# One slot of 512 edges in each edge stage fetched row by row by ScalarE's DMAs instead of GpSimd's gathers

## The chip, the cores and the metric

The kernel runs on one core of one Trainium2 chip. The metric is the device time of one execution in microseconds. Every profile here is of one execution; its span runs from the first to the last instruction, and the execution's own time is a little longer.

## What the kernel computes

A graph network of four layers over 6250 nodes of 128 features and 100,000 edges that are sorted by destination. `x` is normalised per row and clipped at zero; two layers of the first kind follow, then a residual, the same normalisation, two layers of the second kind and a last residual.

```python
def _gine_layer(x, src, dst, edge_attr, W1l, b1l, gl, bl, W2l, b2l):   # layers 0 and 1
    msg = relu(x[src] + edge_attr)
    agg = segment_sum(msg, dst, num_segments=6250)
    h = (x + agg) @ W1l + b1l
    h = (h - mean(h)) * rsqrt(var(h) + 1e-5) * gl + bl
    return relu(relu(relu(h) @ W2l + b2l))

def _gin_conv(x, edge_index, wA, bA, wB, bB, eps):                      # layers 2 and 3
    agg = segment_sum(x[src], dst, num_segments=6250)
    return relu(((1 + eps) * x + agg) @ wA.T + bA) @ wB.T + bB
```

What matters here is `x[src]` in layers 0 and 1: for each of the 100,000 edges one row of 512 bytes is fetched from a table of node rows in DRAM, and the edge's own 512 bytes are added to it.

## The kernel before, in words

Layers 0 and 1 are the two edge stages. Each walks over all edges in 49 turns (`TURNS`) of four slots (`SLOTS`); a slot is 512 edges, four (`EPP`) on each of 128 partitions. The turns are numbered through both stages, 0 to 97; `n % TURNS` is the turn within its stage. For each slot:

- **GpSimd** (line 566) issues four gathers. Each is an indirect DMA that fetches 128 rows, one per partition, by a column of row numbers from `src_all`. Two turns of buffers (`xg`) exist; before each half of a turn GpSimd waits until the sums of the same half two turns earlier are made. In the first two turns the rows come from the raw input, later from the table in DRAM, which SyncE wrote (`table_written`).
- **SyncE** loads the edges' own features for a turn (`ea`, lines 463 and 467), three turns ahead, and stores finished count units (line 482).
- **ScalarE** copies a slot's edge features into PSUM (`stage_attributes`, line 641), one slot ahead: the copy for slot i+1 is made once the sum of slot i is there. After the last slot of a half it clips both slots at zero (`messages`, line 646). After that, in turns in which a count unit is due, it casts one out of PSUM (`units_out`, line 633).
- **VectorE** adds the gathered rows to the staged features (`slot_sum`, line 968) once the copy and the gathers of that slot have landed (`gathered`). Between the sums it builds 0/1 matrices for counts (line 960), which later layers use. Between the last sum of a turn and the first of the next it adds finished windows into the accumulator (line 885), for which it reads column numbers into registers (line 907), and builds the turn's 0/1 matrix of destinations (line 932).
- **TensorE** multiplies the messages by the destinations' matrix (`edge_windows`, line 1333), one half of a turn at a time, 16 matmul instructions each, and the counts' matrices (line 1317).

After the last turn of a stage VectorE adds the last windows and the layer's two products run (line 1418 is the first). The next stage's gathers wait for the new table.

Layers 2 and 3 fetch only the edges that the counts don't cover, with indirect DMAs at line 586, and keep a tile `product` of 128 x 480 numbers for the counts' results.

The order on each engine is the program's order; an engine waits on counting semaphores. A DMA adds 16 to its semaphore when it has landed.

Of the kernel before, what the change touches and what calls it, by code (L numbers as in the profile page):

```python
# [16 lines left out]
P = 128  # L17
NODES = 6250
EDGES = 100000
D = 128  # L20
EPP = 4
SUP = P * EPP
# [3 lines left out]
SLOTS = 4  # L26
TURNS = SUPERS // SLOTS
HALVES = (range(0, 2), range(2, SLOTS))
# [7 lines left out]
GROUPS = -(-BLOCKS // GB)  # L36
# [9 lines left out]
CW = 40  # L46
# [33 lines left out]
UPG = 12  # L80
KEPT = (LEFT_PAIRS + 1) * UPG
RING = 3
CELL_RING = 6
EDGE_TURNS = 2 * TURNS
RAW_TURNS = 2
RAW_CHUNKS = SLOTS * EPP

LAYER_UNITS = [min(range(UNITS), key=lambda k: abs(2 * UNIT_END[k] - CHUNKS)) + 1, UNITS]
LAYER_CHUNKS = [0] + [UNIT_END[k - 1] for k in LAYER_UNITS]
COUNT_TURNS = TURNS - 1 - RAW_TURNS  # L90

# [9 lines left out]
def slot_chunks(n, u):  # L101

    chunks = turn_chunks(n)
    return [c for i, c in enumerate(chunks) if 1 + i * (SLOTS - 1) // len(chunks) == u]


def units_in(chunks):

    return [UNIT_OF[c] for c in chunks if c + 1 in UNIT_END]


def hots(n):
# [41 lines left out]
def gnn_kernel(nc, x, src, dst, edge_attr, W1, b1, gamma, beta, W2, b2,  # L154
               w1a, b1a, w1b, b1b, eps1, w2a, b2a, w2b, b2b, eps2, out):
    with ExitStack() as ctx:
        ctx.enter_context(nc.allow_non_contiguous_dma(reason="columns of biases"))

        def sb(name, shape, dt=F32):
            return ctx.enter_context(nc.sbuf_tensor(name, shape, dt))  # L160

        def sem(name):
            return ctx.enter_context(nc.semaphore(name))
# [4 lines left out]
        table = nc.dram_tensor("node_table", [PADDED, D], F32, kind="Internal").ap()  # L168
# [34 lines left out]
        src_all = sb("src_all", [P, SUPERS + SLOTS, EPP], I32)  # L203
# [37 lines left out]
        xg = sb("xg", [P, 2, SLOTS, EPP, D])  # L241
# [11 lines left out]
        cells = cell_room[:, 0:CELL_RING * CB].rearrange("p (r c) -> p r c", c=CB)  # L253
        counts = [cell_room[:, 0:UPG * HALF_B * CW].rearrange("p (s c) -> p s c", s=UPG),
                  hid[:, :].bitcast(F16)[:, 0:UPG * (BLOCKS - HALF_B) * CW].rearrange("p (s c) -> p s c", s=UPG)]
        product = sb("product", [P, UPG, CW])
        count_out = sb("count_out", [P, 2, CB], F16)

        xp_room = sb("xp_room", [P, BLOCKS * PARTS * D], BF16)
# [11 lines left out]
        ea = xp_room[:, RING0:RING0 + 2 * RING * SLOTS * EPP * D].bitcast(F32).rearrange(  # L271
            "p (t u j d) -> p t u j d", t=RING, u=SLOTS, j=EPP)
# [6 lines left out]
        ea_stage = psG[:, 3, 0:EPP * D]  # L279
# [36 lines left out]
        table_written = sem("table_written")  # L316
# [26 lines left out]
        raw_centred = sem("raw_centred")  # L343
        raw_step = sem("raw_step")
        gathered = [[sem(f"gathered{q}_{u}") for u in range(SLOTS)] for q in range(2)]
        ea_staged = sem("ea_staged")
        ea_loaded = [sem(f"ea_loaded{t}") for t in range(RING)]
        summed = sem("summed")
# [51 lines left out]
        def uses_before(layer, q, pairs):  # L400

            return (layer - 2) * (pairs + (1 - q))
# [135 lines left out]
        @block.gpsimd  # L538
        def _(pool):
            nc.gpsimd.memset(rows_x[:, BLOCKS - 1, :], 0.0).then_inc(pad_cleared, 1)  # L540
            nc.gpsimd.memset(acc[:, PADDED:ACC], 0.0).then_inc(consts_made, 1)
            nc.gpsimd.memset(small_eps[:, :], LN_EPS).then_inc(consts_made, 1)
            nc.gpsimd.memset(ident[:, :], 0.0).then_inc(consts_made, 1)
            pool.wait_ge(consts_made, 3)
            nc.gpsimd.affine_select(out=ident[:, :], in_=ident[:, :], compare_op=ALU.not_equal, fill=1.0,
                                    base=0, pattern=[[-1, P]], channel_multiplier=1).then_inc(consts_made, 1)
            nc.gpsimd.iota(iota_c[:, :], pattern=[[1, IOTA]], base=0, channel_multiplier=0).then_inc(more_consts, 1)
            nc.gpsimd.iota(round_off[:, :], pattern=[[WIN, BLOCKS + 1]], base=0, channel_multiplier=0,
                           allow_small_or_imprecise_dtypes=True).then_inc(more_consts, 1)
            nc.gpsimd.memset(ones_row[:, :], 1.0).then_inc(more_consts, 1)  # L550
            pool.wait_ge(src_ready, 2)
            for layer in range(2):

                if layer == 1:
                    pool.wait_ge(table_written, 16 * GROUPS * 2)
                for n in range(layer * TURNS, (layer + 1) * TURNS):
                    if n == RAW_TURNS:
                        pool.wait_ge(table_written, 16 * GROUPS)
                    for u in range(SLOTS):
                        h = u // len(HALVES[0])  # L560
                        if n >= 2 and u == HALVES[h][0]:

                            pool.wait_ge(summed, (n - 2) * SLOTS + HALVES[h][-1] + 1)
                        for j in range(EPP):
                            s = (n % TURNS) * SLOTS + u
                            nc.gpsimd.indirect_dma_start(  # L566
                                xg[:, n % 2, u, j, :], None, x if n < RAW_TURNS else table,
                                bass.IndirectOffsetOnAxis(ap=src_all[:, s, j:j + 1], axis=0),
                            ).then_inc(gathered[n % 2][u], 16)
            rounds = load_rounds(pool)  # L570
            skipped, pairs, use = load_plan(pool)
            for layer in range(2, LAYERS):

                pool.wait_ge(table_written, 16 * GROUPS * (layer + 1))

                def turn(k, q):

                    m = pool.snap(k + uses_before(layer, q, pairs))

                    pool.wait_ge(idx_ready[q], pool.snap(k + groups_before(layer, pairs) + 1))  # L580

                    pool.wait_ge(reduced[q], pool.snap(m * rounds + 1))
                    pool.sem_inc(slots_opened, 1)
                    for u in range(SLOTS):
                        for j in range(EPP):
                            nc.gpsimd.indirect_dma_start(  # L586
                                xg[:, q, u, j, :], None, table,
                                bass.IndirectOffsetOnAxis(ap=idx[:, q, u, j:j + 1], axis=0),
                            ).then_inc(row_gathered[q][u // len(HALVES[0])], 16)

                with pool.Fori(0, pairs) as k:
                    turn(k, 0)
                    turn(k, 1)
                turn(pairs, 0)
# [3 lines left out]
        def _(act):  # L598
            act.sem_inc(products_out, 1)

            for half in range(2):
                rows = (FIRST, SECOND)[half]
# [24 lines left out]
            def units_out(chunks):  # L627

                for k in units_in(chunks):
                    act.wait_ge(cells_used, UNIT_END[k])  # L630
                    if k >= 2:
                        act.wait_ge(count_stored[k % 2], 16 * (k // 2))
                    act.copy(count_out[:, k % 2, :], psA[:, :, :].rearrange("p k c -> p (k c)")[:, 0:CB]  # L633
                             ).then_inc(count_evicted, 1)

            def stage_attributes(i):
# [3 lines left out]
                    act.wait_ge(ea_loaded[n % RING], 32 * (n // RING + 1))  # L640
                act.copy(ea_stage, ea[:, n % RING, u, :, :].rearrange("p j d -> p (j d)")).then_inc(ea_staged, 1)  # L641

            def messages(n, slots):

                half = ea[:, n % RING, slots[0]:slots[-1] + 1, :, :].rearrange("p u j d -> p (u j d)")
                act.activation(half, half, ACT.Relu).then_inc(msg_ready, 1)  # L646

            def edges(layer):
                start = RAW_TURNS if layer == 0 else layer * TURNS
                for n in range(layer * TURNS, start):  # L650
                    for slots in HALVES:
                        act.wait_ge(summed, n * SLOTS + slots[-1] + 1)
                        messages(n, slots)
                act.wait_ge(windows_cleared, 2 * (layer + 1))
                stage_attributes(start * SLOTS)
                for n in range(start, (layer + 1) * TURNS):
                    for slots in HALVES:
                        for u in slots:
                            i = n * SLOTS + u
                            act.wait_ge(summed, i + 1)  # L660
                            if i + 1 < (layer + 1) * TURNS * SLOTS:
                                stage_attributes(i + 1)
                            if u == slots[-1]:
                                messages(n, slots)
                            units_out(slot_chunks(n, u))

            def first_indices(layer):

# [123 lines left out]
        def _(dve):  # L792
# [171 lines left out]
            def slot_sum(n, u):  # L964

                dve.wait_ge(ea_staged, (n - RAW_TURNS) * SLOTS + u + 1)
                dve.wait_ge(gathered[n % 2][u], 16 * EPP * (n // 2 + 1))
                nc.vector.tensor_tensor(ea[:, n % RING, u, :, :].rearrange("p j d -> p (j d)"), ea_stage,  # L968
                                        xg[:, n % 2, u, :, :].rearrange("p j d -> p (j d)"),
                                        ALU.add).then_inc(summed, 1)  # L970

            def edges(layer):
# [169 lines left out]
            for h, rows in halves:  # L1142
                f = flt[0:rows, 2 + h, :]
# [385 lines left out]
```

## Time and profile before

| | us |
|---|---|
| median of three runs | 2780.12 |
| lowest, highest | 2774.67, 2780.39 |
| profiled execution, its own time | 2776.51 |
| its span | 2774.5 |
| GpSimd busy | 1948.0 (70%) |
| TensorE busy | 1915.5 (69%) |
| VectorE busy | 1712.8 (62%) |
| ScalarE busy | 744.9 (27%) |

Busy times add up an engine's own instructions; register, branch, wait and DMA-issuing instructions are not in them and stand under names with a q (DVEq is VectorE's sequencer, SPq SyncE's). The two edge stages take the stretches from about 110 to 1005 us and from about 1040 to 2029 us of the span.

### The profile page before, as it was taken

To read this page: it belongs to the slowest core of one execution; us is meant where nothing else is said; L and a number is where in the kernel's file an instruction comes from. 1 tells how busy PE (TensorE), PEld (TensorE's weight loads), DVE (VectorE), ACT (ScalarE), POOL (GpSimd) and SP (SyncE) were. 2 spreads that over 40 slices of the span, in tenths; PEclk is the share of its full clock that TensorE was granted. 3 is DMA by queue.
4 is the path that set the end of the run, shared out by engine and by line. 5 is a ranking of instruction groups with operands and counts; after the bars stand their busy time and mean duration, and the time that the engine had idled before them with its cause. 6 is when DMAs were issued, how large, how long until landed. Compare 5 with 4: busy or idle time off the path is not lost.

```text
span 2774.5 us, 30336 instructions
## 1 busy us (share of the span) xinstructions
PE 1915.5 (69%) x9233; PEld 1265.2 (46%) x9233; DVE 1712.8 (62%) x2755; ACT 744.9 (27%) x1002; POOL 1948.0 (70%) x2060
## 2 busy tenths in 40 slices
PE   3566565656665672656565666665678999989999
PEld 2444444434444442434343444433444565545656
DVE  7887777777776754777677767777764212442223
ACT  4222222222223241333333333333362000220001
POOL 6777777777777727777777777777706777367773
PEclk8788787777778886888778888888778999999999
DMA  6344333343434332444444444544425665466653
GB/s 198 113 128 120 113 112 115 116 125 113 128 112 143 120 116 85 121 149 128 142 135 150 134 151 148 162 152 157 142 83 193 222 211 199 140 205 214 219 191 115
DMA packets 224861, 403.74 MB, mean 146 GB/s; under 512 B 41224, under 2 KB 129116, under 8 KB 224740
## 3 DMA queue, kind: packets, MB, share of 16 engines
q1 hardware_dynamic: 159204, 267.94, 28.0%
q0 software_dynamic: 65536, 134.35, 18.3%
q8 instruction: 56, 0.92, 0.1%
q14 instruction: 65, 0.53, 0.1%
HBM read 337.92 MB, written 64.21 MB: 145 GB/s over the span
## 4 chain that ended last, share of the span: by engine, by line
POOL 47%; PE 26%; issue 17%; DVE 6%; DMA 3%; DVEq 1%; ACT 1%; POOLq 0%; SPq 0%; ACTq 0%
POOL xg L566 47%; PE psA L1354 17%; PE psG L1369 4%; DMA xg<-node_table,src_all 3%; PE psG L1418 2%; PE psA L1426 1%; DVE cell_room L960 1%; DVE xp_room L968 1%; DVEq L907 1%; DVE acc L885 0%; PE psG L1333 0%; PE psG L1448 0%; DVE xp_room L949 0%; DVE hid L932 0%; DVE hid L1065 0%
## 5 line engine op out<-in xcount | busy, mean ns | idle before, releaser
L566 POOL DMA_INDIRECT xg<-node_table,src_all x1536 | 1450.9, 945 | 513.5 <-issue 462.0
L1333 PE MATMUL psG<-hid,xp_room 128*128 128x160 f32 x3072 | 611.3, 374 | 414.0 <-DVE hid L932 400.8
L1333 PEld LDWEIGHTS psG<-hid,xp_room 128*128 128x128 f32 x3072 | 591.4, 253 | 466.1 <-issue 453.7
L1317 PE MATMUL psA<-cell_room,xp_room 128*128 128x512 f16 (+1 forms) x2176 | 552.4, 406 | 335.9 <-ACT count_out L633 247.8
L960 DVE TENSOR_SCALAR cell_room<-psG,cell_all 128x980 f16<-128x980 int16 x1088 | 712.2, 712 | 0.0
L586 POOL DMA_INDIRECT xg<-node_table,idx x480 | 461.2, 961 | 256.6 <-issue 253.2
L641 ACT COPY psG<-xp_room 128x512 f32<-128x512 f32 x384 | 226.4, 590 | 1246.7 <-DVE xp_room L968 1228.9
L968 DVE TENSOR_TENSOR xp_room<-psG,xg 128x512 f32<-128x512 f32 x384 | 261.9, 682 | 403.4 <-DMA xg<-node_table,src_all 399.0
L1317 PEld LDWEIGHTS psA<-cell_room,xp_room 128*128 128x128 f16 x2176 | 215.2, 104 | 629.8 <-ACT count_out L633 281.3
L885 DVE TENSOR_TENSOR acc<-acc,product 128x40 f32 x192 | 39.0, 203 | 395.3 <-ACT product L693 371.7
L932 DVE SCALAR_TENSOR_TENSOR hid<-loc_all,round_off,psG 128x2560 f32<-128x2560 f32 x96 | 274.7, 2861 | 0.0
L1354 PE MATMUL psA<-cell_room,xp_room 128*128 128x480 f16 x1200 | 248.9, 369 | 21.8 <-DVE xp_room L1071 21.8
L1354 PE MATMUL psA<-hid,xp_room 128*128 128x480 f16 x1152 | 235.9, 366 | 0.0
L646 ACT ACTIVATE xp_room<-xp_room 128x1024 f32<-128x1024 f32 x196 | 206.0, 1052 | 12.9 <-DVE xp_room L968 8.9
L885 DVE TENSOR_TENSOR acc<-acc,psG 128x160 f32 x272 | 87.2, 320 | 190.3 <-issue 143.8
L633 ACT CAST count_out<-psA 128x1960 f16<-128x1960 f32 x96 | 171.3, 1784 | 72.6 <-PE psA L1317 72.5
L1354 PEld LDWEIGHTS psA<-cell_room,xp_room 128*128 128x128 bf16 x1200 | 118.1, 99 | 147.5 <-issue 26.5
L1354 PEld LDWEIGHTS psA<-hid,xp_room 128*128 128x128 bf16 x1152 | 112.7, 98 | 118.2
L1369 PE MATMUL psG<-rows_h,xg 128*128 128x160 f32 x960 | 135.3, 299 | 0.0
L1369 PEld LDWEIGHTS psG<-rows_h,xg 128*128 128x128 f32 x960 | 133.7, 190 | 3.5
L693 ACT COPY product<-psA 128x480 f32<-128x480 f32 x16 | 8.9, 558 | 420.5 <-PE psA L1354 420.5
L1024 DVE SCALAR_TENSOR_TENSOR rows_h<-loc_all,round_off,psG 128x2560 f32<-128x2560 int16 x30 | 86.4, 2879 | 0.0
(145 smaller groups left out, 794.3 us busy)
## 6 DMA issues: line engine op xcount, KB each, us to landing
xp_room<-in_edge_attr_dram SPq DMA_DIRECT2D x98, 768.0 KB, 4.8
cell_room<-count_store SPq DMA_DIRECT2D x16, 3000.0 KB
count_store<-count_out SPq DMA_DIRECT2D x96, 490.0 KB, 3.2
hid<-count_store SPq DMA_DIRECT2D x16, 2880.0 KB
xp_room<-in_edge_attr_dram SPq DMA_DIRECT2D x98, 256.0 KB, 5.1
xg<-node_table,src_all POOLq DMA_INDIRECT x1536, 2.5
node_table<-rows_h SPq DMA_DIRECT2D x48, 256.0 KB, 2.3
xg<-node_table,idx POOLq DMA_INDIRECT x480
```

Source lines behind the costliest of these rows:

```text
L566: nc.gpsimd.indirect_dma_start(xg[:, n % 2, u, j, :], None, x if n < RAW_TURNS else table, bass.IndirectOffsetOnAxis(ap=src_all[:, s, j:j ...
L586: nc.gpsimd.indirect_dma_start(xg[:, q, u, j, :], None, table, bass.IndirectOffsetOnAxis(ap=idx[:, q, u, j:j + 1], axis=0),).then_inc(row_ ...
L633: act.copy(count_out[:, k % 2, :], psA[:, :, :].rearrange("p k c -> p (k c)")[:, 0:CB]).then_inc(count_evicted, 1)
L641: act.copy(ea_stage, ea[:, n % RING, u, :, :].rearrange("p j d -> p (j d)")).then_inc(ea_staged, 1)
L646: act.activation(half, half, ACT.Relu).then_inc(msg_ready, 1)
L932: nc.vector.scalar_tensor_tensor(out=rows.rearrange("p u j w -> p (u j) w"), in0=loc.unsqueeze(2).broadcast_to((P, SLOTS * EPP, WIN)), sca ...
L960: nc.vector.tensor_scalar(cells[:, c % CELL_RING, h * IOTA:(h + 1) * IOTA], iota_bank[:, 0:IOTA], float(h * IOTA), cell_all[:, c:c + 1], A ...
L968: nc.vector.tensor_tensor(ea[:, n % RING, u, :, :].rearrange("p j d -> p (j d)"), ea_stage, xg[:, n % 2, u, :, :].rearrange("p j d -> p (j ...
L1317: last = nc.tensor.matmul(psA[:, bank, 0:w], src_hot[:, hots(n) % 2, i, :], cells[:, c % CELL_RING, c0:c0 + w], start=(c == first), stop=( ...
L1333: last = nc.tensor.matmul(psG[:, q, h * WIN:(h + 1) * WIN], ea[:, t, u, j, :], rows[:, u, j, :], start=(u == slots[0] and j == 0), stop=(u ...
L1354: last = nc.tensor.matmul(out_cols, xp[:, b, part, :], counts[h][:, :, i * CW:(i + 1) * CW], start=(b == 0 and part == 0), stop=(b == BLOC ...
L1369: last = nc.tensor.matmul(psG[:, q, h * WIN:(h + 1) * WIN], xg[:, q, u, j, :], late_hot[:, q, u * EPP + j, :], start=(u == slots[0] and j ...
```

## The change

One slot, number 2, of the last turn of each stage is no longer gathered by GpSimd. Its 512 rows are fetched by 512 DMAs of one row each, which ScalarE issues during turns 2 to 44 of the same stage: after its other work for each of the slots 0, 1 and 2 it loads four row numbers into registers and issues four DMAs, which fill one partition of a new tile `row_slot`. All of them count up one semaphore, and VectorE waits for its full count before it sums that slot. The waits of GpSimd and the counts of `gathered` follow. `product` becomes a view of `row_slot`.

```diff
+ROW_SLOT = 2
+ROW_TURNS = (TURNS - 1,)
+ROW_STARTS = (2,)
+ROW_STEP = 3
...
+def by_rows(n, u):
+    return u == ROW_SLOT and n % TURNS in ROW_TURNS
+
+def landed(n, u):
+    return sum(not by_rows(t, u) for t in range(n % 2, n + 1, 2))
...
-        product = sb("product", [P, UPG, CW])
+        row_slot = sb("row_slot", [P, EPP * D])
+        product = row_slot[:, 0:UPG * CW].rearrange("p (s c) -> p s c", s=UPG)
...
+        row_landed = [sem(f"row_landed{k}") for k in range(len(ROW_TURNS))]
...
                     for u in range(SLOTS):
+                        if by_rows(n, u):
+                            continue
                         h = u // len(HALVES[0])
-                        if n >= 2 and u == HALVES[h][0]:
+                        if n >= 2 and u == min(v for v in HALVES[h] if not by_rows(n, v)):
...
+            def gather_rows(layer, n, u):
+                p = (n % TURNS - ROW_STARTS[0]) * ROW_STEP + u
+                if not 0 <= p < P or u >= ROW_STEP:
+                    return
+                if p == 0:
+                    act.wait_ge(table_written, 16 * GROUPS * (layer + 1))
+                s = ROW_TURNS[0] * SLOTS + ROW_SLOT
+                _, rows = nc.values_load_multi_w_load_instructions(
+                    src_all[p:p + 1, s, :], [mybir.EngineType.Activation], min_val=0, max_val=NODES - 1,
+                    skip_runtime_bounds_check_because="the load checks its address against the table itself")
+                for j, row in enumerate(rows):
+                    act.dma_start(row_slot[p:p + 1, j * D:(j + 1) * D],
+                                  table[bass.DynSlice(row, 1), :]).then_inc(row_landed[0], 16)
...
                             units_out(slot_chunks(n, u))
+                            gather_rows(layer, n, u)
...
-                dve.wait_ge(gathered[n % 2][u], 16 * EPP * (n // 2 + 1))
-                nc.vector.tensor_tensor(ea[:, n % RING, u, :, :].rearrange("p j d -> p (j d)"), ea_stage,
-                                        xg[:, n % 2, u, :, :].rearrange("p j d -> p (j d)"),
+                rows = xg[:, n % 2, u, :, :].rearrange("p j d -> p (j d)")
+                if by_rows(n, u):
+                    k, rows = ROW_TURNS.index(n % TURNS), row_slot[:, :]
+                    dve.wait_ge(row_landed[k], 16 * SUP * (n // TURNS + 1))
+                else:
+                    dve.wait_ge(gathered[n % 2][u], 16 * EPP * landed(n, u))
+                nc.vector.tensor_tensor(ea[:, n % RING, u, :, :].rearrange("p j d -> p (j d)"), ea_stage, rows,
                                         ALU.add).then_inc(summed, 1)
```

## Rows read from the trace of the kernel before

**Rows 1.** The page's chain that ended last, by engine: shares of the span.

```profile
POOL 47%; PE 26%; issue 17%; DVE 6%; DMA 3%; DVEq 1%; ACT 1%; POOLq 0%; SPq 0%; ACTq 0%
```

**Rows 2.** The page's groups: count, busy us, mean ns, idle us before, releaser.

```profile
L566 POOL DMA_INDIRECT xg<-node_table,src_all x1536 | 1450.9, 945 | 513.5 <-issue 462.0
```

**Rows 3.** Waits: engine, line, waited for, us in total, times, longest us.

```profile
ACT psG L641 <- DVE xp_room L968: 1228.9, 365, 8.4
...
DVE xp_room L968 <- DMA xg<-node_table,src_all: 399.0, 191, 6.9
```

**Rows 4.** Windows of 100 us inside both stages; last columns clock, DMA share, GB/s.

```profile
core 0: us, PE busy (x) PEld busy (x) DVE busy (x) ACT busy (x) POOL busy (x), PEclk, DMA share, GB/s
...
410.00:510.00 100.00, 64.50 (x302) 45.21 (x302) 74.41 (x108) 25.49 (x33) 75.51 (x80) 0.79 0.39 116
...
1740.00:1840.00 100.00, 61.21 (x280) 41.31 (x280) 69.97 (x102) 37.47 (x40) 75.61 (x81) 0.83 0.52 163
```

**Rows 5.** Timeline across a turn's border: start us, us, instruction, idle before.

```profile
400.36 0.69 DVE L968 TENSOR_TENSOR xp_room<-psG,xg 128x512 f32<-128x512 f32 x1 [3.08 <-DMA xg<-node_table,src_all]
...
406.83 0.67 DVE L968 TENSOR_TENSOR xp_room<-psG,xg 128x512 f32<-128x512 f32 x1
...
407.53 0.59 ACT L641 COPY psG<-xp_room 128x512 f32<-128x512 f32 x1 [4.87 <-DVE xp_room L968]
```

**Rows 6.** Timeline of stage one's last turn.

```profile
989.47 0.59 ACT L641 COPY psG<-xp_room 128x512 f32<-128x512 f32 x1 [0.76 <-DVE xp_room L968]
...
991.64 2.34 PE L1333 MATMUL psG<-cell_room,xp_room 128*128 128x160 f32 x16
...
993.17 0.69 DVE L968 TENSOR_TENSOR xp_room<-psG,xg 128x512 f32<-128x512 f32 x1 [3.73 <-DMA xg<-node_table,src_all]
...
995.56 0.94 POOL L566 DMA_INDIRECT xg<-node_table,src_all  x1 [0.30 <-issue]
998.24 0.69 DVE L968 TENSOR_TENSOR xp_room<-psG,xg 128x512 f32<-128x512 f32 x1 [4.38 <-DMA xg<-node_table,src_all]
998.96 1.06 ACT L646 ACTIVATE xp_room<-xp_room 128x1024 f32<-128x1024 f32 x1 [4.48 <-DVE xp_room L968]
...
1000.07 4.35 PE L1333 MATMUL psG<-cell_room,xp_room 128*128 128x160 f32 x16 [6.10 <-ACT xp_room L646]
```

**Rows 7.** Windows of that turn's end, columns as in rows 4.

```profile
994.00:996.00 2.00, 0.00 (x0) 0.00 (x0) 0.00 (x0) 0.48 (x1) 1.39 (x3) 1.00 1.00 386
...
1000.00:1002.00 2.00, 1.93 (x7) 1.93 (x8) 0.48 (x2) 0.02 (x1) 0.00 (x0) 0.50 0.01 4
```

**Rows 8.** Timeline of stage two's last turn.

```profile
2022.17 0.69 DVE L968 TENSOR_TENSOR xp_room<-psG,xg 128x512 f32<-128x512 f32 x1 [4.33 <-DMA xg<-node_table,src_all]
...
2024.00 4.38 PE L1333 MATMUL psG<-cell_room,xp_room 128*128 128x160 f32 x16 [5.38 <-ACT xp_room L646]
```

**Rows 9.** Sequencer instructions of lines 396, 907 and 494: count, min/median/max ns.

```profile
L396 ACTq TENSOR_LOAD <-plan_i x1: 587/587/587, 2080.1 to 2080.1; - x1
L396 ACTq FUSED_REGOPS  x1: 157/157/157, 2080.7 to 2080.7; - x1
...
L907 DVEq TENSOR_LOAD <-first_i x272: 296/304/974, 84.1 to 2717.9; - x136
...
L494 SPq FUSED_REGOPS  x28: 42/50/151, 2113.0 to 2703.8; - x28
L494 SPq DMA_DIRECT2D cell_room<-count_store x16: 377/378/398, 2032.4 to 2685.0; - x16
```

**Rows 10.** Timeline of SyncE at the start of the span.

```profile
2.00 13.01 SPq L438 DMA_DIRECT2D rows_x<-in_x_dram  x12
...
20.53 0.43 SPq L448 DMA_DIRECT2D bias_first<-in_L_gnn_b_dram  x1
```

**Rows 11.** The chain in order of time, at the turn's border: start us, us, what.

```profile
400.76 0.31 DVEq L907
```

## The prediction

> **What bounds the kernel now.** I read the page's chain of waits first: GpSimd's gathers (line 566) carry 47% of the span and "issue" another 17% [rows 1]. The page's groups tell what that is: 1536 gathers of 945 ns, each behind 0.30 us of issue (462.0 / 1536), so one gather leaves GpSimd every 1.245 us and a turn of 16 takes 19.9 us [rows 2]. The waits by engine confirm that the others follow: VectorE (line 968) stands 399.0 us for landed gathers, 4.2 us in each of the 96 turns, and ScalarE's staging copy (line 641) stands 1228.9 us for VectorE's sums [rows 3]. The stage table shows how steady this is: GpSimd is busy 75.5 and 75.6 of 100 us while the DMA engines' share goes from 0.39 to 0.52, and ScalarE works only 25 to 37 of 100 us [rows 4]. So in the two edge stages each gather removed is worth 1.245 us, as long as the sums stay on GpSimd's heels at the last turn, and ScalarE has most of its time free.
>
> **What goes.** Slot 2 of the last turn of both stages: 4 gathers each, 4 x 1.245 = 4.98 us. What is late next? In the last turn of stage one the last gather goes out at 995.56, the sum of slot 3 starts at 998.24 and the message after it at 998.96 [rows 6]. With four gathers fewer that gather goes out at 990.58 and its sum can start at 993.26. Ahead of it stand two things. The sum of slot 2 needs only the copy staged at 989.47 to 990.06 [rows 6], since its rows landed four turns earlier, so it runs at about 990.1 instead of 993.17. The copy for slot 3 then stands behind a message of 1.05 us on ScalarE and is done by about 991.7. Neither reaches 993.26: the whole 4.98 us arrives. TensorE is free too, its first half of the turn ends at 991.64 + 2.34 = 993.98 [rows 6], and the second half's message is ready at 998.96 + 1.06 - 4.98 = 995.04.
>
> **A second gain behind it.** TensorE's second half (16 matmuls) took 4.35 us in stage one and 4.38 us in stage two, against 2.34 us for the same 16 in the first half [rows 6, 8]. The granted clock says why: 1.00 (2.4 GHz) at 994 to 996, 0.50 (1.2 GHz) at 1000 to 1002, after TensorE had been idle since 993.98 [rows 7]. With the message 4.98 us earlier TensorE is idle for 1.1 us instead of 6.1, and in the rows the clock was still full 2.0 us after its last matmul. So the half should take 2.34: 2.0 us more per stage. The window adds of VectorE wait for exactly this half, and VectorE has read its column numbers by then (two loads, 1.3 us after the adds before), so I let the 2.0 stand. It is an estimate from rows at both clocks; the other end is 0.
>
> **What comes: ScalarE's row work.** 128 slots in turns 2 to 44 of each stage each get one load of four row numbers and four DMAs of 512 B: 512 DMAs a stage, 1024 in all. Before's trace has no DMA issued by ScalarE, so I price it by neighbours. A register load on ScalarE took 0.587 us, with 0.157 us of register work behind it; on VectorE 272 loads had a median of 0.304 [rows 9]. A DMA at a computed address on SyncE (line 494) took 0.378 us with 0.050 of register work [rows 9]; a small parameter DMA 0.43 us [rows 10]. With 0.05 us between sequencer instructions:
> - mid: 0.6 + 3 x 0.35 for the loads, 4 x (0.05 + 0.43 + 0.10) for the DMAs: X = 4.0 us per slot;
> - low: one load of 0.3 for all four numbers, 4 x 0.38: 1.8 us;
> - high: 4 x (0.59 + 0.16 + 0.08) and 4 x 1.35, where 1.08 is what each of the 12 feature loads at the start took, back to back (13.01 / 12) [rows 10], and the rest register work: 8.7 us. Those loads move 256 KB each, a row 0.5 KB, so I stay near line 494.
>
> What does X touch? ScalarE's order is copy for slot i+1 (after sum i), perhaps a message, perhaps the 1.8 us cast of a count unit, then the row work of slot i. No row work follows slot 3. The sequencer goes on while the datapath computes: on VectorE a register load starts at 400.76 inside the sum of 400.36 to 401.05 [rows 5, 11]. So row work hides behind copies and messages. Two loops can close in a turn. (a) Row work of slots 0 and 1 delays the copies of slots 2 and 3, and then VectorE needs from one turn's sum 3 to the next sum 0 6.47 us (400.36 to 406.83 [rows 5]) plus copy and sum, 1.28: 2X + 7.75. (b) Row work of all three and one copy and sum: 3X + 1.3. Both stay under 19.9 as long as X is under 6.1 us. At X = 4.0 they are 15.8 and 13.3. So the forecast does not move with X from 1.8 to 6.1: a single copy may come a microsecond late, but GpSimd waits only for sums of two turns before (two turns of 19.9, less the 10 of a half and the 2.7 of a landing: some 27 us of play), and turns 45 to 48 carry no row work and let VectorE catch up by 4.2 us each. I cost the row work at nothing; its cover is ScalarE's wait of 1228.9 us.
>
> The Trainium skill (DMA: Bandwidth & Descriptors, Latency and other measured facts) gives a register load from memory a floor of about 600 ns. The median of 304 [rows 9] is half of it, the single ScalarE load of 587 agrees with it. By the page X would be an estimated 4.7: the sum stays, but it lies beyond the point of the milder form of rival 2 below.
>
> The other added waits: VectorE's wait for the 512 rows stands at the last turn, the last row goes out in turn 44, some 80 us earlier, so it costs nothing; nothing queues behind it. ScalarE's wait for the table stands at turn 2, where GpSimd waits for the same count. The tile that now holds both rows and products is written in different stages.
>
> **Sum.** 2 x (4.98 + 2.0) = 14 us. The profiled execution took 2776.5 (span 2774.5 and 2.0 around it): 2762.5. The median of the three runs is 3.6 above it, which would give 2766. I take 2764.
>
> **Rivals.**
> 1. *Only the gathers count* (the clock is down again at the second half, or the window adds hold it): 2 x 4.98 = 10, so 2766 to 2770. For it: the clock of that stretch is 0.50 in both stages now. Against: the 1.1 us of idle.
> 2. *ScalarE becomes the bound: slower.* It decides at X = 6.1. Above it VectorE falls behind by 2(X - 6.1) per turn for 43 turns; four turns give 16.6 back and the forecast's 7 per stage is spent, so the point of no gain is 6.1 + 23.6 / 86 = 6.4 us. At X = 6.6 it is 2 x (86 x 0.5 - 16.6 - 7) = +39, 2815. A milder form has the same place: if ScalarE's sequencer can't run ahead of its datapath, two copies, a message and a cast (4.0 us) add to loop (a), which then decides at X = 4.1 and loses from 4.4; at 4.5, 2 x (34.4 - 23.6) = +22, 2798. At the high end, 8.7, loop (b) takes 27.4 a turn: 2 x (43 x 7.5 - 23.6) = +598. For it: the load of 0.587 and the 1.08 of the feature loads [rows 9, 10]. Against: row 11's overlap and line 494's 0.378.
>    The Trainium skill (DMA: Bandwidth & Descriptors, Rules for kernel authors) speaks against the change: coalesce small transfers, since under 64 KB one pays mostly overhead. If the overhead were paid in ScalarE's order it would be this rival, with a time by the size of that overhead; line 494 issues in 0.378, and no row of before has a transfer of one row from ScalarE.
> 3. *GpSimd's pace suffers*, its descriptors or its gathers meeting 1024 more DMAs: slower from 14 / 1024 = 0.014 us per row DMA on; at 0.03 it is +17, 2794. Against: 75.5 and 75.6 busy at shares of 0.39 and 0.52 [rows 4].
> 4. *Swallowed*: VectorE or ScalarE is still a few us behind at the last turn (X of 6.25 to 6.4, or the milder form at 4.3), and the sums no longer end with the gathers: 2774 to 2780.
>
> **Numbers.** Forecast 0.54, rival 1 0.22, rival 4 0.09, rival 2 0.11, rival 3 0.04. A measurement of this kernel tells a change from none at about 0.2% (5.6 us): faster 0.76, same 0.09, slower 0.15. Range 2757 to 2778: below, three us for the runs' spread and a shorter gap at TensorE; above, rival 1 and most of rival 4.
>
> **What would show it.** Right: line 566 has 1528 gathers at 945 ns and the same 0.30 of issue; both edge stages are 7 us shorter, of which 5 stand ahead of the last sum and 2 in the second half's matmuls at clock 1.00; ScalarE's DMAs take 0.4 us each, 1024 of them; VectorE's wait for gathers stays near 4 us a turn. Wrong: line 566 shows waits for VectorE's line 968, the copy at line 641 stops waiting for VectorE and VectorE waits for it, or a gather takes more than 945 ns.

## The result and the profile after

The changed kernel takes 2769.02 us (median of five runs, 2764.28 to 2770.69) against 2780.39 before (now five runs, with the three of the table ahead of the prediction among them): 11.4 us less, ratio 0.9959 with a 95% interval of [0.9948, 0.9971]. Forecast were 2764, a range of 2757 to 2778, and faster by more than 0.2%. The profiled execution took 2769.02, its span 2766.7; against the span of before that is 7.8 us less, so a single pair of profiles shows two thirds of what the medians show. The profiled execution before lies 3.9 us under its median, the one after is the median.

The page's groups after, columns as in [rows 2]. They answer to [rows 2] and to the staging copy in [rows 3]; line 584 is the old 566, 659 the old 641, 1007 the old 968, 679 the old 646, 919 the old 885, 1371 the old 1333, 1456 the old 1418, 479 and 483 the old 463 and 467. The later runs shift them by a few lines more.

```profile
L584 POOL DMA_INDIRECT xg<-node_table,src_all x1528 | 1443.2, 945 | 513.7 <-issue 458.8
...
L659 ACT COPY psG<-xp_room 128x512 f32<-128x512 f32 x384 | 226.3, 589 | 1244.0 <-DVE xp_room L1007 1216.2
```

Eight gathers fewer, the rest at the same 945 ns and 458.8 / 1528 = 0.30 us of issue. ScalarE's copies wait for VectorE's sums as long as before (1216.2 us against 1228.9).

The row work itself, by line: one register load for all four numbers in each visit (line 669) and four DMAs (line 673); count, then min/median/max ns. In the page's table of DMA queues the new queue has 2048 packets for 1024 DMAs (columns: packets, MB, share of the 16 engines).

```profile
L669 ACTq TENSOR_LOAD <-src_all x256: 480/489/1630, 89.8 to 1931.5; - x128
...
L673 ACTq FUSED_REGOPS  x1024: 37/37/48, 90.3 to 1933.3; - x171
L673 ACTq MOVE row_slot<-node_table x1024: 29/29/38, 90.4 to 1933.7; - x171
L673 ACTq DMA_DIRECT2D row_slot<-node_table x1024: 213/214/513, 90.5 to 1933.7; - x171
```

```profile
q10 hardware_dynamic: 2048, 0.53, 0.1%
```

One visit (the row work behind one slot), in the timeline after: four DMAs take 1.55 us from 408.01 to 409.56. The register load ahead of them starts at 407.4 and takes 0.49 us, under the copy of 407.36 to 407.95.

```profile
407.36 0.59 ACT L659 COPY psG<-xp_room 128x512 f32<-128x512 f32 x1 [4.87 <-DVE xp_room L1007]
...
408.01 1.55 ACTq L673 DMA_DIRECT2D row_slot<-node_table  x4
```

So X is about 2.2 us (407.36 to 409.56), near the low end of the forecast's 1.8 to 8.7 and half its middle of 4.0.

**Stage two's end** went as forecast. It answers to [rows 8]: the last gather is issued at 2012.25, its sum starts 2.60 later, and the second half's 16 matmuls take 2.44 us instead of 4.38.

```profile
2012.25 0.94 POOL L584 DMA_INDIRECT xg<-node_table,src_all  x1 [0.30 <-issue]
...
2014.85 0.69 DVE L1007 TENSOR_TENSOR xp_room<-psG,xg 128x512 f32<-128x512 f32 x1 [2.43 <-DMA xg<-node_table,src_all]
2015.58 1.06 ACT L679 ACTIVATE xp_room<-xp_room 128x1024 f32<-128x1024 f32 x1 [2.41 <-DVE xp_room L1007]
2016.69 2.44 PE L1371 MATMUL psG<-cell_room,xp_room 128*128 128x160 f32 x16 [1.26 <-ACT xp_room L679]
...
2020.21 10.79 PE L1456 MATMUL psG<-acc,w_first 128*128 128x512 f32 x26 [1.09 <-DVE acc L919]
```

**Stage one's end** did not. It answers to [rows 6]. The last gather leaves at 990.55, 5.01 us earlier, as forecast. But its sum starts only at 995.99, 5.44 us after the issue instead of 2.68, and so only 2.25 us earlier than before. SyncE had issued the load of 1 MB of edge features for turn 50 at 990.49 and 990.91, in the same microsecond as the gather. In the profiles of before, of after and of e1, e3, e4 and e5 that load follows within 0.04 us the end of the 32 matmuls of the turn before, which release its buffer. They ended 1.34 us earlier than before the change, so both moved: the gather by 5.01, the load from 991.83 to 990.49. TensorE then stood idle for 4.2 us and ran the second half in 4.11 us.

```profile
990.13 0.69 DVE L1007 TENSOR_TENSOR xp_room<-psG,row_slot 128x512 f32<-128x512 f32 x1 [0.66 <-ACT psG L659]
990.49 0.38 SPq L479 DMA_DIRECT2D xp_room<-in_edge_attr_dram  x1
990.55 0.94 POOL L584 DMA_INDIRECT xg<-node_table,src_all  x1 [0.30 <-issue]
990.91 0.49 SPq L483 DMA_DIRECT2D xp_room<-in_edge_attr_dram  x1
...
991.23 2.41 PE L1371 MATMUL psG<-cell_room,xp_room 128*128 128x160 f32 x16 [0.77 <-ACT xp_room L679]
995.99 0.69 DVE L1007 TENSOR_TENSOR xp_room<-psG,xg 128x512 f32<-128x512 f32 x1 [5.16 <-DMA xg<-node_table,src_all]
996.71 1.06 ACT L679 ACTIVATE xp_room<-xp_room 128x1024 f32<-128x1024 f32 x1 [5.14 <-DVE xp_room L1007]
...
997.82 4.11 PE L1371 MATMUL psG<-cell_room,xp_room 128*128 128x160 f32 x16 [4.18 <-ACT xp_room L679]
...
1003.03 10.79 PE L1456 MATMUL psG<-acc,w_first 128*128 128x512 f32 x26 [1.09 <-DVE acc L919]
```

From the profiles, then: the first product of stage one comes at 1003.03 instead of 1005.52 (2.5 us earlier), that of stage two at 2020.21 instead of 2029.47 (9.3 earlier, so 6.8 from stage two). From there to the end of the span the kernel takes 746.5 us (2766.7 - 2020.21) instead of 745.0 (2774.5 - 2029.47), which gives 1.5 back. 9.3 - 1.5 = 7.8.

### The profile page after: what moved, and what is told of

Same layout as the page of the kernel before. It is cut to its first block, busy times and chain, and to the rows that moved or that the text cites. A ratio compares the mean times of both kernels' runs of the same rounds, so it can differ in the third digit from the quotient of the medians.

```text
span 2766.7 us, 33658 instructions
## 1 busy us (share of the span) xinstructions
PE 1910.3 (69%) x9233; PEld 1259.2 (46%) x9233; DVE 1712.1 (62%) x2755; ACT 745.7 (27%) x1002; POOL 1940.3 (70%) x2052
## 3 DMA queue, kind: packets, MB, share of 16 engines
q10 hardware_dynamic: 2048, 0.53, 0.1%
## 4 chain that ended last, share of the span: by engine, by line
POOL 47%; PE 25%; issue 17%; DVE 5%; DMA 4%; DVEq 1%; ACT 1%; ACTq 0%; POOLq 0%; SPq 0%
POOL xg L584 47%; PE psA L1392 17%; PE psG L1407 4%; DMA xg<-node_table,src_all 3%; PE psG L1456 2%; PE psA L1464 1%; DVE xp_room L1007 1%; DVE acc L919 0%; DVEq L941 0%; DVE cell_room L994 0%; PE psG L1486 0%; DVE hid L1103 0%; PE psA L1473 0%; DVE xp_room L844 0%; DVE xp_room L983 0%
## 5 line engine op out<-in xcount | busy, mean ns | idle before, releaser
L584 POOL DMA_INDIRECT xg<-node_table,src_all x1528 | 1443.2, 945 | 513.7 <-issue 458.8
L659 ACT COPY psG<-xp_room 128x512 f32<-128x512 f32 x384 | 226.3, 589 | 1244.0 <-DVE xp_room L1007 1216.2
L919 DVE TENSOR_TENSOR acc<-acc,row_slot 128x40 f32 x192 | 39.1, 204 | 396.7 <-ACT row_slot L727 373.2
L727 ACT COPY row_slot<-psA 128x480 f32<-128x480 f32 x16 | 8.9, 558 | 426.7 <-PE psA L1392 426.7
```

Source lines behind the costliest of these rows:

```text
L584: nc.gpsimd.indirect_dma_start(xg[:, n % 2, u, j, :], None, x if n < RAW_TURNS else table, bass.IndirectOffsetOnAxis(ap=src_all[:, s, j:j ...
```

## The experiments

Each was timed beside the kernel before on its own chip, and its ratio is to that.

**e1: the changed kernel again** (no edit), what the next three are compared with.

> The changed kernel once more, as the anchor of this group. Theory: its rows are hidden, stage two gave the whole 7 us of the forecast and stage one only 2.5, because the last gather of stage one, issued at 990.55, shared the DMA engines with the edge load that SyncE issued at 990.49 and landed only at 995.99. Expected 2766 to 2770 us, ratio to before 0.995 to 0.9965; in stage one's last turn the last gather takes 5 us to its sum again and the second half's 16 matmuls 4.1 to 4.4 us. Rival (the lost time is chance of one execution): the stage one half takes about 2.4 us here.

Measured: 2769.19 us (2767.06 to 2770.56), ratio 0.9961 [0.9947, 0.9974]. The last turn of stage one repeats the picture: load at 990.63, gather at 990.69, sum at 996.18, second half 4.10 us. So the lost time isn't one execution's chance.

**e2: the load held until the last sum of stage one.**

```diff
                         sp.wait_ge(scattered[n % 2], sp.snap(rounds * (n // 2 + 1) + 1))
+                        if n == TURNS - 2:
+                            sp.wait_ge(summed, TURNS * SLOTS)
                         load_turn(n + RING)
```

> The changed kernel, with SyncE's load for turn 50 (issued in turn 47 of stage one) held until the last sum of stage one is made. Theory (the load delays the last gather, and the longer idle time drops TensorE's clock): the last gather of stage one is summed 2.7 us after its issue, the second half runs at the full clock in 2.4 us, the first product of stage one comes 4 to 5 us earlier than in the changed kernel; 4 to 5 us below the repeat, about 2763. Rival 1 (landing is slow for another reason, such as HBM): no difference to the repeat. Rival 2 (landing improves, the clock falls anyway): 2.7 us less. Rival 3 (the held load makes stage two's start late): stage two's first sums wait for edge features.

Measured: 2765.40 us (2764.93 to 2766.99), ratio 0.9949 [0.9935, 0.9963]: 3.8 us below the repeat. The intervals of the two ratios overlap, but all five runs lie under all five of e1 (2766.99 the highest here, 2767.06 the lowest there). The timeline of stage one's last turn:

```profile
992.01 0.95 POOL L586 DMA_INDIRECT xg<-node_table,src_all  x1 [0.31 <-issue]
...
994.57 0.69 DVE L1009 TENSOR_TENSOR xp_room<-psG,xg 128x512 f32<-128x512 f32 x1 [2.38 <-DMA xg<-node_table,src_all]
995.29 1.06 ACT L681 ACTIVATE xp_room<-xp_room 128x1024 f32<-128x1024 f32 x1 [2.36 <-DVE xp_room L1009]
995.34 0.38 SPq L479 DMA_DIRECT2D xp_room<-in_edge_attr_dram  x1
...
996.40 2.44 PE L1373 MATMUL psG<-cell_room,xp_room 128*128 128x160 f32 x16 [1.40 <-ACT xp_room L681]
...
999.94 2.41 PE L1458 MATMUL psG<-acc,w_first 128*128 128x512 f32 x5 [1.10 <-DVE acc L921]
```

The gather is summed 2.56 us after its issue and the half takes 2.44. From the last gather to the first product it is 7.93 us instead of 12.48: 2.9 of these 4.5 us are the landing, 1.7 the matmuls at the higher clock. Rivals 1 and 2 of the expectation don't fit that; rival 3 doesn't show either, the first gather of stage two leaves 36.65 us after the first product of stage one (1036.59 - 999.94), 36.64 in the changed kernel.

One thing weakens this profile, not the five runs. The last gather itself left 1.5 us later here (992.01 instead of 990.55), and the 32 matmuls that release the load ended at 992.77. Without the hold the load would have come 0.8 us behind the gather in this execution, and they might not have met. So the profile shows a clean end beside one that meets the load; what the hold is worth stands in the medians alone.

The granted clock in a window of two microseconds at the start of the second half, columns as in [rows 4] (the clock is the third number from the end): first the changed kernel (second half from 997.82), then this one (from 996.40):

```profile
998.00:1000.00 2.00, 2.00 (x8) 2.00 (x9) 0.32 (x1) 0.00 (x0) 0.00 (x0) 0.50 0.02 4
```

```profile
996.00:998.00 2.00, 1.60 (x12) 1.60 (x12) 0.64 (x2) 0.35 (x1) 0.00 (x0) 1.00 0.36 125
```

Idle for 4.2 us TensorE came back at 0.50 (1.2 GHz), idle for 1.4 us at 1.00 (2.4 GHz).

**e3: the row DMAs without the skip.**

```diff
-                        if by_rows(n, u):
-                            continue
...
-                if by_rows(n, u):
-                    k, rows = ROW_TURNS.index(n % TURNS), row_slot[:, :]
-                    dve.wait_ge(row_landed[k], 16 * SUP * (n // TURNS + 1))
-                else:
-                    dve.wait_ge(gathered[n % 2][u], 16 * EPP * landed(n, u))
+                if by_rows(n, u):
+                    dve.wait_ge(row_landed[0], 16 * SUP * (n // TURNS + 1))
+                dve.wait_ge(gathered[n % 2][u], 16 * EPP * landed(n, u))
```

> The row DMAs alone: ScalarE issues all 1024, VectorE waits for their count, but GpSimd gathers all slots and the sum uses the gathered rows. Theory (row work of 2.2 us a slot hides under ScalarE's waits and disturbs nothing): same as before, ratio 0.999 to 1.001, 1536 gathers at 945 ns and 1.245 us apart. Rival (row DMAs slow GpSimd's gathers or their landing, or ScalarE's delay reaches the sums): slower than before; at 0.014 us per row DMA it would be +14 us, 1.005.

Measured: 2780.12 us (2776.41 to 2782.32), ratio 1.0001 [0.9992, 1.0010]. All 1024 row DMAs are free within 0.1%, and rival 3 of the prediction (GpSimd's pace) falls.

Its profile also shows the meeting with the load in a kernel that still has all gathers, one slot earlier: slot 2's last gather leaves 0.06 us behind the load and is summed 5.56 us later, while slot 3's, which leaves at 994.50, is summed after 2.60 us and ends the stage. There the meeting costs nothing.

```profile
989.44 0.38 SPq L479 DMA_DIRECT2D xp_room<-in_edge_attr_dram  x1
989.50 0.94 POOL L582 DMA_INDIRECT xg<-node_table,src_all  x1 [0.30 <-issue]
...
995.06 0.69 DVE L1003 TENSOR_TENSOR xp_room<-psG,xg 128x512 f32<-128x512 f32 x1 [6.68 <-DMA xg<-node_table,src_all]
```

**e4: the skip without the row DMAs** (`gather_rows` isn't called, the tile is zero, so the output leaves out the node rows of those edges).

> The skip alone: GpSimd skips the slot, no row DMA is issued and the sum of that slot adds a tile of zeros, so the output leaves out those 512 edges' node rows. Theory: the whole gain is the skip, so it equals the repeat within 2 us (0.9950 to 0.9965 of before). Rival (the row DMAs cost what the median fell short of the 14 us forecast): 2 to 4 us faster than the repeat.

Measured: 2767.62 us (2764.64 to 2770.75), ratio 0.9960 [0.9946, 0.9974], 1.6 us under the repeat with overlapping runs. The whole gain is the skip. In its profile the load fell at 990.95, 1.0 us after the last gather (989.96), and that gather was summed after 2.66 us with a second half of 2.44 us. So with the load 0.06 us ahead of the gather they meet, and with the load a microsecond behind it they don't.

**e5, e6 and e7: two, three and four slots by rows.** `ROW_TURNS` takes the last K turns, and each visit fetches a slot's four rows for every K.

```diff
-ROW_TURNS = (TURNS - 1,)
+ROW_TURNS = tuple(range(TURNS - K, TURNS))
...
+                for k, turn in enumerate(ROW_TURNS):
+                    s = turn * SLOTS + ROW_SLOT
...
+                        act.dma_start(row_slots[k][p:p + 1, j * D:(j + 1) * D],
+                                      table[bass.DynSlice(row, 1), :]).then_inc(row_landed[k], 16)
```

> Two slots by rows in each stage: slot 2 of the last two turns (47 and 48). Each of the 128 visits of ScalarE fetches eight rows; one visit's row work is then 2 x 2.19 = 4.4 us. Theory (two loops per turn, 2X + 7.75 and 3X + 1.3, both under 19.9): they are 16.6 and 14.4, so the second slot gains its 4.98 us a stage as well, 10 us below the changed kernel, near 2759. Rival 1 (a deeper turn loop than I see: VectorE's counts and sums of the last two turns take 15.6 us each and can't keep a pace of 15): 0 to 5 us of gain. Rival 2 (ScalarE's sequencer can't run ahead, the loop closes at X = 4.1): slower than the changed kernel by some 15 us.

Measured: 2764.76 us (2761.93 to 2771.06), the kernel before 2783.47 on this chip, ratio 0.9929 [0.9916, 0.9943]. Against the ratio of one slot that is 0.3% more, some 9 us, near the 10 forecast; the two intervals don't meet. In the profiled execution, the slowest of the five, the end of both stages was less good: stage one met the load again (sum 5.63 us after the issue), and in stage two TensorE ran most of its last 32 matmuls at the low clock (granted 0.50 from 2014 to 2018, 0.65 from 2018 to 2020):

```profile
2014.05 7.20 PE L1372 MATMUL psG<-cell_room,xp_room 128*128 128x160 f32 x32 [4.31 <-ACT xp_room L680]
```

And the second slot brought the last gather of stage one no further forward: it left at 990.47, with one slot at 990.55. GpSimd had lost the time early, in its only long wait for a sum:

```profile
121.06 0.95 POOL L584 DMA_INDIRECT xg<-node_table,src_all  x1 [4.74 <-DVE xp_room L1008]
```

In turn 2, the first with row work, VectorE waits 4.0 us each for two copies of ScalarE (at most 1.7 in the changed kernel), and turn 3's first sum comes at 116.98 instead of 112.45. VectorE has no lead on GpSimd there. That this is what made GpSimd wait is read from the profile; no run separates it.

> Three slots by rows in each stage: slot 2 of turns 46, 47 and 48, twelve rows a visit, X = 6.6 us, just over the 6.1 at which loop (a) is to decide. Theory: 2X + 7.75 = 20.9 a turn, 1.0 over GpSimd's 19.9, for 43 turns = 43 us of lag; the last four turns run at VectorE's own 15.6 instead of 19.9 and give 17 back: 26 us slower a stage, 2780 + 52 = 2832. GpSimd shows waits for VectorE's sums, and ScalarE's copies come late. Rival (ScalarE has more room than the loops say, since sums and copies may slide within a turn): faster than two slots by up to 10, 2749.

Measured: 3016.29 us, ratio 1.0839 [1.0823, 1.0856]. Slower as forecast, but by 233 us instead of the 52 of the expectation. The waits have turned over: ScalarE's copy now waits for its own sequencer ("issue"), VectorE for ScalarE. Columns as in [rows 3]:

```profile
ACT psG L661 <- issue: 1440.1, 256, 6.8
DVE xp_room L1010 <- ACT psG L661: 596.3, 260, 9.9
```

ScalarE's timeline over one turn shows the loop:

```profile
505.10 0.59 ACT L661 COPY psG<-xp_room 128x512 f32<-128x512 f32 x1 [6.47 <-issue]
...
506.58 0.58 ACT L661 COPY psG<-xp_room 128x512 f32<-128x512 f32 x1
507.10 4.18 ACTq L676 DMA_DIRECT2D row_slot<-node_table  x8
512.11 1.55 ACTq L676 DMA_DIRECT2D hid<-node_table  x4
513.71 0.59 ACT L661 COPY psG<-xp_room 128x512 f32<-128x512 f32 x1 [6.55 <-issue]
...
520.74 0.59 ACT L661 COPY psG<-xp_room 128x512 f32<-128x512 f32 x1 [5.46 <-issue]
...
527.82 0.59 ACT L661 COPY psG<-xp_room 128x512 f32<-128x512 f32 x1 [6.49 <-issue]
```

The copies stand 7.13, 7.03 and 7.08 us apart: X is 7.1, not the 6.6 that I had scaled up from 2.19, and three of them and the copy and sum of slot 0 (505.10 to 506.58, 1.48) make 22.7 a turn. The rows fit loop (b). They hardly tell it from (a), which at X = 7.1 would make 21.9 a turn.

> Four slots by rows in each stage: slot 2 of turns 45 to 48, sixteen rows a visit, X = 8.8 us. Theory: loop (b), 3X + 1.3 = 27.7 a turn, is the longer; 43 x 7.8 - 17 = 318 us a stage, 2780 + 636 = 3416. If only loop (a) held, 25.3 a turn, it would be 2780 + 430 = 3210. Rival (ScalarE's busy time alone counts, 5.1 us a turn beside 26.3): 31.4 a turn, 3740.

Measured: 3607.42 us (two runs, 3604.32 and 3610.52), ratio 1.2961 [1.2937, 1.2984], where 3416 were expected. The copies:

```profile
514.42 0.58 ACT L661 COPY psG<-xp_room 128x512 f32<-128x512 f32 x1
...
523.52 0.59 ACT L661 COPY psG<-xp_room 128x512 f32<-128x512 f32 x1 [8.52 <-issue]
...
533.12 0.59 ACT L661 COPY psG<-xp_room 128x512 f32<-128x512 f32 x1 [8.03 <-issue]
...
542.52 0.59 ACT L661 COPY psG<-xp_room 128x512 f32<-128x512 f32 x1 [8.82 <-issue]
...
544.01 0.58 ACT L661 COPY psG<-xp_room 128x512 f32<-128x512 f32 x1
```

They are 9.1, 9.6 and 9.4 apart and the turn 29.6: 3 x 9.37 + 1.49. So both points lie on 3X + 1.5, with X the distance of two copies. That alone is only bookkeeping of one turn; what supports the loop is that the whole kernels' times follow from it. With 86 turns that have row work: 3016 is 233 over before, 2.7 a turn, and 22.7 - 19.9 = 2.8; 3607 is 824 over, 9.6 a turn, and 29.6 - 19.9 = 9.7. Of the 17 us a stage that I let the last turns give back nothing is seen in these sums.

**e8: two slots and the held load.**

> Two slots by rows, and SyncE's load for turn 50 held until the last sum of stage one. Theory: both gains add up: 4 us below the two slots alone where those meet the load at the end of stage one, about 2755. Rival (with two slots the load falls elsewhere and meets nothing): equal to two slots within 1 us.

Measured: 2761.97 us (2761.83 to 2763.96), ratio 0.9926 [0.9913, 0.9940]: the fastest, 2.8 us under two slots alone by the medians, with intervals that overlap. The last turn of stage one is clean: the last 32 matmuls run in 4.65 us and the first product starts at 999.14. Against e2, one slot with the same hold, the ratio is 0.0023 lower (6.4 us, the intervals overlap) and the profiled span 4.5 us shorter; GpSimd loses 3.50 us at 120.84, as in e5. So the second slot is worth some 4 to 9 us, less than its 10.

**e9 to e12: a group on a slower chip.** On the chip of the next four the kernel before takes 3694 us. Gathers and staging copies take what they take elsewhere (in e9 948 and 590 ns); the time lies between the instructions. Many stand apart by "issue", time in which their engine waited for nothing that the profile shows. In e9, the kernel before with the held load, single matmuls of a count unit, which elsewhere follow each other at once, are 0.8 us apart:

```profile
327.27 0.59 PE L1319 MATMUL psA<-cell_room,xp_room 128*128 128x512 f16 x1 [0.81 <-issue]
328.71 0.58 PE L1319 MATMUL psA<-cell_room,xp_room 128*128 128x512 f16 x1 [0.85 <-issue]
```

> The kernel before, with SyncE's load for turn 50 held until the last sum of stage one, as a control of the held load. In the kernel before that load is issued at 991.83, 3.7 us ahead of the last gather, which lands 2.7 us after its issue as in stage two. Theory (the load costs only where it is issued together with the last gather, and the clock there is low for the idle time): same as before, ratio 0.999 to 1.001; the second half still takes 4.3 us. Rival (holding the load is worth 4 us by itself, whatever the gathers): 0.9985.

Measured (e9): 3694.39 us against 3693.96, ratio 0.9998 [0.9984, 1.0011]. The same, as expected, but the stage's end lies elsewhere on this chip (GpSimd waits 568.4 us for sums), so it doesn't test what it was meant to: what the held load does to the kernel before stays untested.

> The two slots by rows of before, and in each visit one more register load and two more row DMAs whose rows nobody uses. A visit took 4.6 us with two slots, 6.94 with three, 9.3 with four, and the turns 22.7 and 29.6 with three and four: 3X + 1.5. Theory: X = 4.6 + 0.54 + 2 x 0.45 = 6.04, the turn 19.6, still under GpSimd's 19.9: same as two slots within 3 us, ratio 0.992 to 0.994. Rival (loop (a), 2X + 7.75, or the casts between visits close it earlier): 2 us or more a turn over, above 2850.

Measured (e10, where two slots and half a slot more are fetched by rows, without the held load): 4101.99 us, ratio 1.1104 [1.1082, 1.1126].

> Two slots by rows in turns 46 and 48 instead of 47 and 48, with the held load. Theory (with neighbours VectorE and TensorE are late at the end: the second half waited for TensorE's first half, not for its message): the turn between gives VectorE back 4 us, 1 to 3 us below the neighbours, near 2760. Rival (the end of the stage is set by the last gather either way): same within 1 us.

Measured (e11, with the held load, `ROW_TURNS = (TURNS - 3, TURNS - 1)`): 3895.91 us, ratio 1.0542 [1.0521, 1.0564].

> Two neighbouring slots with the held load once more, beside the one with slots apart: 2762 us, ratio to before 0.992 to 0.994.

Measured (e12): 3894.32 us, ratio 1.0539 [1.0517, 1.0561]. The same kernel (e8) that is 0.7% faster than before elsewhere is 5.4% slower here. ScalarE's timeline says where: eight row DMAs take 3.88 us in one visit and 13.77 in another, 13 us later.

```profile
504.45 3.88 ACTq L676 DMA_DIRECT2D row_slot<-node_table  x8
...
517.21 13.77 ACTq L676 DMA_DIRECT2D row_slot<-node_table  x8
```

In the chain of that stretch most steps of line 676, register instructions and DMA issues alike, take 0.70 us each, often with another 0.70 of issue behind:

```profile
522.17 0.69 ACTq L676
522.86 0.01 issue
522.87 0.69 ACTq L676
523.56 0.70 issue
524.26 0.70 ACTq L676
```

In that stretch the price goes by the number of instructions, and a two-slot visit has 26 (2 loads, 8 times three). Over the whole kernel the median of its 2048 row DMAs is the usual 0.214 us, so only stretches are slow. All three expectations missed (0.992 to 0.994, about 2760 and 2762 us), and what they were to tell can't be read from these runs: the next half slot costs 208 us (4102 - 3894, of which the missing hold may be 3) in an engine that is already the bound, and slots apart or together make no difference in it. What holds the instructions back isn't shown. The changed kernel itself, with half the instructions, wasn't tried on that chip.

## Why the prediction was right, and where not

- *Gathers at 1.245 us each are the bound, ScalarE has room.* Right. The skip alone gives 0.9960, all of the change's 0.9959.
- *The row work is hidden.* Right for the time: 1.0001 for the rows alone. It is not hidden in the first turn of row work, where two of VectorE's sums wait 1.6 and 1.7 us for their copies (0.7 and 0.8 before) and the first of turn 3 comes 1.8 us later (112.45 instead of 110.69); GpSimd's room took that up. X was 2.2 us, not 4.0. I had four register loads of 0.35 and found one of 0.489 for all four numbers; I had 0.58 for a DMA with its register work and found about 0.4 (1.55 for four). The Trainium skill (DMA: Bandwidth & Descriptors, Latency and other measured facts) has a floor of about 600 ns for such a load; 0.489 lies under it, so the measurement decides.
- *The sequencer runs ahead of the datapath.* Right on ScalarE too, the register load of 407.4 runs under the copy; with two slots, X = 4.65 (e8's copies of 515.42 and 520.07), beyond the milder form's 4.1, the kernel still got faster.
- *The two loops.* (b) fits two points, 3X + 1.5. (a) was not tested: by the prediction's own terms (b) is the longer one from X = 6.45 on, and both slow kernels lie above that. With 3X + 1.5 the threshold is (19.9 - 1.5) / 3 = 6.1, the number of the prediction, from the other loop. It lies between 4.65, where the kernel still gained, and 7.1.
- *Stage two, 4.98 + 2.0.* Right: 6.8 in the profile.
- *Stage one, 4.98 + 2.0.* This is the step that failed: "its sum can start at 993.26". The 2.68 us of landing were taken over from before, though they depend on what SyncE issues meanwhile. The kernel before issued its load 3.7 us ahead of the last gather of 995.56, as a row of its timeline shows that I had not looked for, and the gather was still summed after 2.68. The gather 5.01 us earlier would by itself have left 1.3 us ahead of the load's 991.83; TensorE's matmuls of the turn before ended 1.34 earlier too, and the two met. Why they did wasn't followed up.

```profile
991.83 0.38 SPq L463 DMA_DIRECT2D xp_room<-in_edge_attr_dram  x1
```

  Landing 5.44, then 4.2 us of idle, then the low clock: 2.5 us instead of 7. e2 gives 3.8 us back in the medians by moving the load alone. This was rival 1's place, in one stage, with another cause than the two it names.
- *The total.* 14 forecast, 11.4 by the medians, 7.8 by the profiles. The time fell into the range because the range went as far as rival 1, not because stage one came as reckoned. The 1.5 us that layers 2 and 3 take more in the profile stay open: the kernels with shorter edge stages show 745.8 to 746.9 from stage two's first product to the end, before and the rows alone 745.0 and 745.1.

The Trainium skill (DMA: Bandwidth & Descriptors, Issuing engines are not separate DMA queues) says that spreading DMAs over issuing engines saves only the sequencer's time to start them. These runs agree: that time, 1.245 us a gather on GpSimd, is what the change saves, with TensorE's clock behind it, and e1's last gather was summed 5.49 us after its issue beside SyncE's load, although GpSimd issued it.

## What to carry to other kernels

Work can be moved from an engine whose instruction issue is the bound to one that waits; price it by the loop of waits that it lengthens, not by the engine's busy time: ScalarE was 27% busy and still became the bound at three slots. When a change moves the last transfer of a stage, look up what other queues issue in the new microsecond, and reckon the TensorE clock behind it. And look at the start of a stage too: there the waits that hid the row work later, VectorE's lead on GpSimd, were not there yet. Last, a gain bought with thousands of sequencer instructions can turn: two slots with the held load gained 0.7% on one chip and lost 5.4% on another, where these instructions stood 0.7 us apart in stretches.

## What the hardware showed that I had not expected

- One register load on ScalarE fetches four numbers from SBUF in 0.489 us (median of 256), less than the 0.587 of the one load of a single number on ScalarE before; on VectorE one number takes 0.304 [rows 9].
- A one-row DMA at a computed address costs ScalarE's sequencer 0.214 us, less than the 0.378 of SyncE's large ones [rows 9], and makes two packets.
- A gather of 64 KB (128 rows of 512 B) that leaves within 0.06 us of a load of 1 MB (768 and 256 KB) is summed after 5.4 to 5.6 us (after, e1, e3, e5); with the load 3.7 us ahead or 1.0 us behind it is 2.7 (before, e4).
- One chip ran the kernel before a third slower (3694 us) and two slots with the held load 41% slower (3894 against 2762), with sequencer instructions 0.7 and 1.4 us apart in stretches.
